# Products within the chunks run after the last value projection instead of before it, next to the following unit's slot products

## The reference

```python
x = x + attention(layernorm(x), Wq, Wk, Wv, Wg, Ws, Wo, g_norm_weight)
x = x + ffn(layernorm(x), gate_w, up_w, down_w, gate_scale, up_scale, down_scale)

# attention, for each of 16 heads (keys 64 wide, values 128, 64 slots):
s = clip(x @ Ws, -32, 32); z = cumlogsumexp(s over time); p = exp(s - z); g = exp(z_prev - z)
hk = hk * g + k (x) p;   ok = q . hk          # first pass over time
hv = hv * g + p (x) v;   o  = softmax(ok) . hv # second pass over time
o = o * rsqrt(mean(o^2) + 1e-5) * g_norm_weight * silu(x @ Wg);   result = o @ Wo
# ffn: (silu(x @ fp8(gate_w) * gate_s) * (x @ fp8(up_w) * up_s)) @ fp8(down_w) * down_s
```

## Time and profile before

| | |
|---|---|
| median of 3 runs | 1321.95 us (1321.73 to 1322.69) |
| the profiled execution | 1322.3 us, span 1320.5 us, granted clock of TensorE 1.0 of full speed |
| PE busy | 1311.0 us, 99% of the span |
| DVE, ACT, POOL busy | 80%, 33%, 12% |
| first block of a far unit to the next (units 13 to 16) | 32.1 us |

### The profile page before, as it was taken

The page is one execution under the profiler, slowest core; times in us unless marked ns, Lnnn a source line. Parts: engine busy times, 40 slices in busy tenths (PEclk is TensorE's granted clock), DMA queues, the critical chain, the costliest instruction groups (busy, mean ns, idle before and its releaser), DMA issues.

```text
span 1320.5 us, 24287 instructions
## 1 busy us (share of the span) xinstructions
PE 1311.0 (99%) x9251; PEld 1096.0 (83%) x9251; DVE 1052.1 (80%) x1686; ACT 433.0 (33%) x1290; POOL 153.3 (12%) x114
## 2 busy tenths in 40 slices
PE   9999999999999999999999999999999999999998
PEld 8788888888888888888888888888888888888887
DVE  8988888988898888888888898889778876755354
ACT  5434223322332233233323332333333333232222
POOL 3222001200120021002101110121110010000000
PEclk9999999999999999999999999999999999999999
DMA  6766556655755575556555755565436654120000
GB/s 204 156 134 163 126 116 147 141 120 120 163 126 128 112 170 121 126 116 166 126 135 117 177 122 121 123 158 127 91 70 145 178 158 79 56 41 32 0 32 33
DMA packets 566560, 157.69 MB, mean 119 GB/s; under 512 B 412848, under 2 KB 557616, under 8 KB 566448
## 3 DMA queue, kind: packets, MB, share of 16 engines
q1 hardware_dynamic: 566448, 156.19, 51.2%
HBM read 92.35 MB, written 63.77 MB: 118 GB/s over the span
## 4 chain that ended last, share of the span: by engine, by line
PE 94%; DVE 2%; issue 1%; DMA 1%; SPq 1%; ACT 1%; POOL 0%; DVEq 0%; ACTq 0%
PE bank L557 20%; PE bank L558 19%; PE bank L559 19%; PE bank L117 13%; PE bank L1888 6%; PE bank L802 4%; PE bank L785 2%; PE bank L648 2%; PE bank L628 2%; PE bank L728 2%; PE bank L637 2%; PE bank L790 1%; PE bank L659 1%; PE bank L1903 0%; PE bank L668 0%
## 5 line engine op out<-in xcount | busy, mean ns | idle before, releaser
L557 PE MATMUL bank<-wvg_hi,xT_hi 128*128 128x512 f32 x512 | 205.7, 402 | 0.0
L559 PE MATMUL bank<-wvg_hi,xT_lo 128*128 128x512 f32 x512 | 199.8, 390 | 0.0
L558 PE MATMUL bank<-wvg_lo,xT_hi 128*128 128x512 f32 x512 | 199.7, 390 | 0.0
L874 ACT ACTIVATE a_and_v<-bank 128x256 f32<-128x256 f32 x128 | 49.2, 384 | 363.4 <-PE bank L559 363.4
L1189 POOL TENSOR_TENSOR rstd<-ssq,neg_half 128x8 f32<-128x8 f32 x32 | 52.4, 1638 | 546.7 <-DVE ssq L1302 546.7
L557 PEld LDWEIGHTS bank<-wvg_hi,xT_hi 128*128 128x128 f32 x512 | 96.2, 188 | 21.6
L559 PEld LDWEIGHTS bank<-wvg_hi,xT_lo 128*128 128x128 f32 x512 | 96.1, 188 | 20.3
L558 PEld LDWEIGHTS bank<-wvg_lo,xT_hi 128*128 128x128 f32 x512 | 96.3, 188 | 18.0
L1246 DVE RECIPROCAL cT<-cT 128x512 f32<-128x512 f32 x32 | 107.1, 3346 | 0.0
L1363 DVE TENSOR_TENSOR y<-y,bank 128x512 f32<-128x512 f32 x128 | 84.8, 677 | 22.7 <-PE bank L559 22.7
L557 PE MATMUL bank<-wo_hi,oT_hi 128*128 128x512 f32 x256 | 99.9, 390 | 0.7 <-issue 0.6
(11 more groups left out here) (190 smaller groups left out, 3024.2 us busy)
## 6 DMA issues: line engine op xcount, KB each, us to landing
o_transposed<-o SPq DMA_DIRECT2D x27, 512.0 KB, 3.6
oT_lo<-o_transposed SPq DMA_DIRECT2D x108, 128.0 KB, 3.1
fp_weights<-q SPq DMA_DIRECT2D x28, 318.0 KB, 3.1
e_tokens<-k_tok_then_wT SPq DMA_DIRECT2D x31, 256.0 KB, 2.5
e_tok<-e_tokens SPq DMA_DIRECT2D x124, 64.0 KB, 2.3
c_tokens<-cT SPq DMA_DIRECT2D x31, 256.0 KB, 2.4
cT<-c_tokens SPq DMA_DIRECT2D x124, 64.0 KB, 2.3
w_slots<-p SPq DMA_DIRECT2D x28, 256.0 KB, 2.3
```

The costliest lines, as they stand in the source:

```text
L557: pe.matmul(dst, w_hi, m_hi, start=(k == 0), stop=False)
L558: pe.matmul(dst, w_hi, m_lo, start=False, stop=False)
L559: last = pe.matmul(dst, w_lo, m_hi, start=False, stop=(k == n - 1))
L874: return act.activation(dst, src, ACT.Copy)
```

## The change

For the units in `JOINED` (2 to 26) the products within chunks of unit u-1 move from between VG2 and VG3 to behind VG3, where unit u begins, and ST of nu, which stood there, moves behind the block. Engines follow: DVE scales the outputs (`times_gate`) and ACT takes the squares of unit u-1 at the start of unit u, ACT with the three `key_state` copies between the two halves of the squares; DVE's `clip`, the low halves of the next pair's weights and `out_norm` move behind the subtraction of the maximum, `out_norm` behind `far_lo`. The squares' unused output goes to `o` instead of a bank. ACT's `split_vg` moves behind the `key_state` copies in every unit with i=3, JOINED or not (unit 27 has i=3 and is not JOINED). In the last unit two of the key sums come later. Of the low halves of batches 2 and 3, POOL makes six instead of eight and later, DVE makes two in unit 1.

```diff
--- before.py
+++ after.py
@@ -55,6 +55,7 @@
 FAR = UNITS - B - 2
+JOINED = range(2, FAR + 1)
 W_FAR = range(2, UNITS - 2)
@@ -254,7 +255,7 @@
     ffn.place(projected=s_job, out_w_read=s_wl, weights_split=s_vgh, vg_lo=(s_vgl, s_vgl2), q_read=s_ok,
-              k_read=s_kb, scores=s_a, e_read=s_hvd, weights_done=s_b, w_ready=s_wm, inter_done=s_oi,
+              k_read=s_kb, scores=s_a, e_read=s_hvd, keys_read=s_hkd, weights_done=s_b, w_ready=s_wm, inter_done=s_oi,
               w_transposed=s_trw, gated=s_oev, gates=s_g, out_transposed=s_tro, out_done=s_y, added=s_ya,
@@ -421,7 +422,7 @@
             if v == 0:
-                sp.wait_ge(s_xl2, 2 * CH)
+                sp.wait_ge(s_xl2, CH + 2)
             if v:
@@ -592,8 +593,11 @@
                 pe.wait_ge(s_xl, 2 * CH)
-            elif j == ST and 1 < u < B:
-                pe.wait_ge(s_xl2, CH * (b - 1))
+            elif j == ST and u == 2:
+                pe.wait_ge(s_xl2, CH)
+            elif j == ST and u == 3:
+                pe.wait_ge(s_xl, 2 * CH + 2)
+                pe.wait_ge(s_xl2, CH + 2)
             if j in (ST, QT, KTJ):
@@ -648,6 +652,15 @@
 
+        def inner_o(u, par):
+
+            for a in range(2):
+                pe.wait_ge(s_bm, 2 * u + a + 1)
+                for c in range(CH):
+                    mm = pe.matmul(O[a][:, c * P:(c + 1) * P], av[par][:, a, c, 0, :], av[par][:, a, c, 1, :],
+                                   start=False, stop=(c == CH - 1), skip_group_check=True)
+                mm.then_inc(s_o, 1)
+
         def inter_ok(u):
@@ -697,7 +710,9 @@
 
-            if not last:
+            if u in JOINED:
+                inner_o(u - 1, 1 - par)
+            elif not last:
                 job(ST, nu, ni)
@@ -718,9 +733,10 @@
             inner_ok(par, (0, 1))
-            key_sums(u, 1)
+            if not last:
+                key_sums(u, 1)
             inner_ok(par, (2, 3))
-            key_sums(u, 2)
+            key_sums(u, 1 if last else 2)
             pe.wait_ge(s_v, (u + 1) * CH)
@@ -728,7 +744,11 @@
             mm.then_inc(s_hvd, 1)
+            if last:
+                key_sums(u, 2)
             inter_ok(u)
+            if u in JOINED:
+                job(ST, nu, ni)
             if u > FAR + 1:
@@ -796,12 +816,8 @@
 
-            for a in range(2):
-                pe.wait_ge(s_bm, 2 * u + a + 1)
-                for c in range(CH):
-                    mm = pe.matmul(O[a][:, c * P:(c + 1) * P], av[par][:, a, c, 0, :], av[par][:, a, c, 1, :],
-                                   start=False, stop=(c == CH - 1), skip_group_check=True)
-                mm.then_inc(s_o, 1)
+            if nu not in JOINED:
+                inner_o(u, par)
             if last:
@@ -942,7 +958,7 @@
             if v == 0:
-                act.wait_ge(s_xl2, 2 * CH)
+                act.wait_ge(s_xl, 2 * CH + 2)
             for a in range(2):
@@ -953,13 +969,14 @@
                 act.wait_ge(s_rstd, u)
-            if not a and u <= FAR:
+            if not a and u <= FAR and u + 1 not in JOINED:
                 act.wait_ge(s_bm, 2 * (u + 1))
...
                 head = O[a][:, c * P:(c + 1) * P]
-                unused = head if a else A[1][:, c * P:(c + 1) * P] if u <= FAR else o[:, a, c, :]
+                unused = head if a else (
+                    A[1][:, c * P:(c + 1) * P] if u <= FAR and u + 1 not in JOINED else o[:, a, c, :])
                 act.activation(unused, head, ACT.Square,
@@ -986,12 +1003,16 @@
             projections, outputs = split_next(u, i, tail)
+            if u in JOINED:
+                head_squares(u - 1, 0)
+            for c in range(CH - 1):
+                key_state(u, c)
+            if u in JOINED:
+                head_squares(u - 1, 1)
             if i == 3 and not tail:
...
                     split_vg(pair_of_next(u), k)
-            for c in range(CH - 1):
-                key_state(u, c)
             if not last:
@@ -1049,8 +1070,9 @@
                 evac(VG2, nu, ni)
-            head_squares(u, 0)
-            head_squares(u, 1)
+            if nu not in JOINED:
+                head_squares(u, 0)
+                head_squares(u, 1)
             if not last:
@@ -1157,7 +1179,8 @@
             if u == 1:
-                for t in range(3 * CH, 4 * CH):
+                pool.wait_ge(s_scan, 3)
+                for t in range(3 * CH + 2, 4 * CH):
                     far_x_lo(t)
@@ -1172,6 +1195,10 @@
                     lo(pair * 5 + 4 + a, wol[:, a, :], woh[:, a, :], stage[:, :])
+                    if first and a == 0:
+                        pool.wait_ge(s_scan, 2)
+                        for t in range(2 * CH + 2, 3 * CH):
+                            far_x_lo(t)
 
@@ -1198,7 +1225,7 @@
         norm_rsqrt(3, 4)
-        for t in range(2 * CH, 3 * CH):
+        for t in range(2 * CH, 2 * CH + 2):
             far_x_lo(t)
@@ -1254,6 +1281,12 @@
             dve.transpose(turn_tile[t - 2 * CH], turn_tile[t - 2 * CH]).then_inc(s_xb, 1)
+
+        def far_x_lo(t):
+
+            dve.wait_ge(s_xh, t + 1)
+            cols = slice(t * P, (t + 1) * P)
+            lo(xl[:, :, cols], landing[t % CH].rearrange("p (k t) -> p k t", k=KT), xh[:, :, cols]).then_inc(s_xl, 1)
 
@@ -1409,17 +1442,22 @@
             nu, ni = u + 1, i + 1
-            if i == 3 and not tail:
+            if u in JOINED:
+                times_gate(u - 1, i - 1, 1)
+                times_gate(u - 1, i - 1, 0)
+            elif i == 3 and not tail:
                 for k in range(2):
                     lo_vg(pair_of_next(u), k)
-            if not last:
+            if not last and u not in JOINED:
                 clip(nu, ni)
...
                     add_y(FAR, c)
-            if not first:
+            if not first and u not in JOINED:
                 out_norm(u - 1)
             value_states(u)
+            if u in JOINED:
+                mean_square(u - 1)
             if first:
@@ -1441,11 +1479,18 @@
                               ALU.subtract).then_inc(s_sub, 1)
+            if u in JOINED:
+                clip(nu, ni)
+                if i == 3:
+                    for k in range(2):
+                        lo_vg(pair_of_next(u), k)
             if u > FAR + 1 and not last:
...
             v = product_of(u)
+            if u in JOINED:
+                out_norm(u - 1)
             if not last:
@@ -1475,6 +1520,9 @@
                 ffn.late_aggregate(dve, 0)
+            if u == 1:
+                for t in range(3 * CH, 3 * CH + 2):
+                    far_x_lo(t)
             if not last:
@@ -1490,6 +1538,14 @@
                 return
+            if nu in JOINED:
+                c_turn(nu)
+                mask_scores(nu, ni)
+                quantise(u, slice(2, 4))
+                gate(2, nu, ni)
+                quantise(u, slice(4, Q8_STEPS))
+                gate(3, nu, ni)
+                return
             if not tail:
@@ -1497,10 +1553,10 @@
                 norm_turn((0, 1))
+            gate(2, nu, ni)
+            times_gate(u, i, 1)
             if tail and i == 2:
                 norm_lo((2, 3))
-            gate(2, nu, ni)
-            times_gate(u, i, 1)
             if not tail:
@@ -1816,6 +1872,7 @@
         sp.wait_ge(w["e_read"], UNITS)
+        sp.wait_ge(w["keys_read"], (CH - 1) * UNITS)
         load_down(2)
...
         load_down(3)

```

## The result

The changed kernel takes 1334.51 us (median of 4 runs, 1331.16 to 1335.41) against 1321.84 for the kernel before, measured beside it: ratio 1.0091, 95% interval 1.0079 to 1.0103. (Two executions of the runs further down, one of e9 at 4631.79 us and one of e10 at 2185.59 us, were of a much slower kind and are left out of every comparison.) The profiled execution has a span of 1332.1 us, against 1320.5: 11.6 us more. The direction was forecast, and the time lies in the range given (1318.5 to 1335), but at its end: the forecast of 1325.0 had 3 us more than before, and 12.7 came. It is the size of the third rival, which had a chance of 0.25; the likeliest case alone had ended at 1328.

A forecast was written before the change was run, and what follows sets the result against it. PE, busy 99% of the span, was taken as the bound. Terms -2.5 (borders) - 2.0 (first units) + 2.7 (unit 27) + 4.8 (k late) = +3.0 gave 1325.0 us; range 1318.5 to 1335, likeliest case 1322 to 1328.

The forecast's parts named there:

- third rival: The loop from w_turn over SP's queue to next k is 0.5 to 1 us longer: about 1333 us; chance 0.25.
- likeliest case: The forecast sum with its own range, 1322 to 1328 us around 1325.0; chance 0.42 including late hk copies.
- Borders: Between small and large products on PE around L802 and the block: 0.10 saved a unit, 2.5 us over 25 units.
- x = 0.09: Assumed cost of the new border from L802's 128x128 to the block's 128x64 products; bounds 0 and 0.35.
- second rival: The border from L802 to L637 costs nothing and k is in time: 4.1 us saved, 1317.9; chance 0.13.
- Copies of hk: ACT's copies between L637 products, behind four squares: no delay taken; bounds 0 and 1.3 us.
- First units: PE's waits in units 1 and 2 shrink, plus 0.2 in unit 26: 2.0 us gained, bounds 0 and 2.0.
- Unit 27: PE's output product waits for DVE's far_lo, delayed by the later split_vg copies: 2.7 us lost, bounds 2.2 and 2.8.
- k late: Later w_turn delays k's load, so PE waits at blocks of i=3 (0.3) and i=4 (0.5): 4.8 us lost.
- c late: The c load has 2.3 of room against a 4.0 move, so p of i=3 is 1.6 us late.
- signs of being wrong: Units growing without a block wait, no unit 27 wait, or PE waiting for p, KTJ's bank or the scores.
- last units: Unit 26 was given 0.2 us gained within the first units' term; the sum had no term for the last unit.

The follow-up runs named there:

- e9: The kernel of e1 with JOINED empty, so all of the change but the joining: 1319.93 us, ratio 0.9990 against the kernel before.
- e10: The kernel of e2 with JOINED starting at unit 4 (units 4 to 26): 1320.18 us, ratio 0.9992 against the kernel before.
- e5: As e2, with PE's order block, L802, ST, ACT's squares behind the hk copies and times_gate behind value_states: 1355.28 us, ratio 1.0267.
- e6: The kernel before with only the move of the low halves of batches 2 and 3 (POOL six and later, DVE two): 1320.31 us, ratio 0.9990.
- e1: The changed kernel with ACT's four split_vg copies ahead of the hk copies in unit 27, as before the change: 1328.17 us, ratio 1.0061.
- e7: As e2, with clip ahead of p in units 2 and 3 alone: 1320.32 us, ratio 0.9990 against the kernel before.
- e8: As e2, with clip ahead of p in all JOINED units: 1322.00 us, ratio 1.0004 against the kernel before.
- e2: As e1, with DVE's out_norm behind w_turn instead of ahead of e_turn: 1321.59 us, ratio 1.0002 against the kernel before.
- e4: As e1, with the steps leading to w_turn first in JOINED units, and far_lo, low halves and out_norm after: 1321.69 us, ratio 0.9998.
- e11: As e2, but out_norm ahead of e_turn in units with i=4 and i=1, as in the changed kernel: 1321.77 us, ratio 1.0004.

## Why the prediction was right in sign and too small in size

- **Borders: mis-sized.** The term was 0.10 a unit, 2.5 us; measured 0.02, 0.5 us. The failed choice is x = 0.09 for the border from L802 to the block, by the entry from ST; it is 0.18. The bounds 0 and 0.35 held it. The second rival (x = 0) is excluded. The Trainium skill (TensorEngine Tiling (Array Packing), Key Properties) states that a change of tiling mode drains TensorE. The trace agrees that the block's entry keeps a price with L802 ahead of it (0.18), and e5's equal sums, 5.19 and 5.20, agree that a change of mode is only moved. But the new entry costs twice the old one's 0.09, and so takes back the 0.10 behind L802 as well, where no mode changed; why is not shown.
- **Copies of hk: right.** 0.65 and 0.66 from one L637 to the next, though ACT has four squares ahead.
- **First units: the number was right by luck.** The 2.0 was meant for the wait in unit 1, those of unit 2 and 0.2 of unit 26. In the trace units 0 and 1 alone gave 2.0, of which 1.1 lie in unit 0, for which the sum had nothing; and e6 has 1.8 of it without any L802 moved. So it is not a wait covered by a later L802: the move of the low halves was the term.
- **Unit 27: mechanism right, mis-sized.** The wait was 2.96 against 2.7, above the bound of 2.8. The 1.8 us of lower clock behind it was missing, and e1 shows that it goes with the wait.
- **k late: the mechanism was right, the agreement in size is luck.** The waits at the block came to 4.4, forecast 4.8, but the forecast had 1.8 ahead of units with i=3 and 3.0 ahead of those with i=4, and the trace has 4.1 and 0.35. `w_turn` was forecast at 12.9, 13.5 and 15.0. Where p starts in time it is 12.9 and, for i=2, 14.1: the copy of the slot weight on ACT costs the 0.5 that the sum had, and the first half of `far_lo` takes 1.37 instead of 0.69 beside POOL's low half of that weight (unit 10), 0.7 that it had not. For i=3 it is 14.3 in the three units where p is 1.1 to 1.3 late, and 15.1 and 15.8 in the others.
- **c late: the step that failed.** The prediction priced c's lateness for i=3 alone, as 1.6 us of p, with every landing at 2.3. p was 1.1 to 3.3 late in i=3, and up to 2.7 late in i=4, 2.4 in i=1 and 2.4 in i=2, which the sum had at nothing. The trace before could have told: there the last c of units with i=4 mostly lands 0.1 to 0.3 after the block and p takes it at 3.2, a room of 3 us, where the prediction itself had `w_turn` of i=3 4.9 late. For QT, the prediction did have `clip` behind p, at 7.05 in i=3, and with 0.69 more that is still in time for QT, which starts 8.3 after the block where nothing is late. With p more than some 2 us late it is not (unit 12, 2.2 late, waits 0.1), and QT waited 3.3 us in all and the output product 1.35, neither of which is in the sum. The signs of being wrong named a wait of PE for p, for KTJ's bank and for the scores, and not the one for ST's bank.
- **The third rival** had the time (6 or 12 us above the forecast, about 1333; measured 9.5 above it), the place (the loop over SP's queue) and, among its grounds, that a p late from c makes the next late too. It put all of the loss into waits at the block, which had only 4.4, and its sign, `w_turn` past 14 and 15.5, came for i=2 and, but for unit 11, not for i=3. For the forecast's step to hold, lateness would have had to end within a unit; the length of the turns (33.3 to 35.5 from i=2) shows why it did not. e7 and e8 show the link to QT by itself, e2 that 1.2 us less up to `w_turn` ends nearly all of the waits.
- **The last units:** 0.4 less in the last unit was not in the sum, and of the 0.5 of unit 26 it had 0.2. Neither needs the joining: unit 26 takes 32.13 in e6 and e9 (32.49 before), and the last unit has its 0.4 in e9.

With the measured sizes the sum is -0.5 - 2.0 + 4.85 + 10.1 - 0.9 = +11.6, the difference of the spans. What remains open is why units 2, 6, 11 and 22 lose most (1.4 to 1.8) and others with the same order nothing. In three of them a slow landing of c or k is to be seen: the last c of unit 6 lands 3.7 us after its issue, that of unit 11 4.1, and the last k for unit 23 3.3, where the median is 2.3 and 2.2. Which other transfer delays them was not tried. The executions of the kernels that wait most also differ more: 1331.16 to 1335.41 in the changed one, 1326.77 to 1334.13 in e1, against 1.6 to 3.6 us from the fastest to the slowest in e2, e4 and e6 to e11.

The best kernels found are e9 and those that tie with it (e6, e7, e10), 1.1 to 1.3 us under the kernel before, at the edge of what can be told (the intervals of e7 and e10 reach 1). Their gain is the low halves', plus at most 0.4 of the last unit.
